# One inverse root moved to GpSimd, a new order of the last part, and first scores ahead of the second head group's projections

## The reference

```
x = x + attn_a(layernorm(x))   # 16 heads of 16; softmax attention for the 307 queries per head
                               # with the largest max(score) - mean(score), zeros for the rest
x = x + ffn(layernorm(x))      # router picks 4 of 16 blocks of 64 hidden channels; relu; biases
x = x + attn_b(layernorm(x))   # rmsnorm, recurrent attention, rmsnorm, gated silu FFN (1024 hidden)
x = x + ffn(layernorm(x))
```

```
S = a_t[..., None] * S + k_t[..., :, None] * v_t[..., None, :]
o_t = einsum('bhk,bhkv->bhv', q_t, S)
mu  = mean(o, -1);  var = mean((o - mu) ** 2, -1)
o   = (o - mu) / sqrt(var + 1e-5)
out = (o * silu(x @ wog.T + bog)) @ wo.T
```

## Time and profile before

| | us |
|---|---|
| median of 3 runs (1687.06 to 1697.72) | 1687.17 |
| the profiled execution, its own time | 1679.56 |
| its span in the trace | 1677.8 |
| PE busy | 1477.8 (88%) |
| DVE busy | 1113.6 (66%) |
| ACT busy | 663.8 (40%) |
| POOL busy | 551.7 (33%) |
| mean granted clock of PE | 0.953 of full |

### The profile page before, as it was taken

The page is one execution under the profiler, slowest core; times in us unless marked ns, Lnnn a source line. Parts: engine busy times, 40 slices in busy tenths (PEclk is TensorE's granted clock), DMA queues, the critical chain, the costliest instruction groups (busy, mean ns, idle before and its releaser), DMA issues.

```text
span 1677.8 us, 25200 instructions
## 1 busy us (share of the span) xinstructions
PE 1477.8 (88%) x8675; PEld 1047.4 (62%) x8724; DVE 1113.6 (66%) x2180; ACT 663.8 (40%) x924; POOL 551.7 (33%) x697
## 2 busy tenths in 40 slices
PE   3688898898898649999988799999999999997898
PEld 2333343343343238888877587878777887876787
DVE  3887778877877775655557667677585857574533
ACT  1275666666675602322232333334333332332111
POOL 5344534544642011422221322332232322331320
PEclk9698999999999959999999999999999999998899
DMA  5222312322222030011010010101010000100000
GB/s 149 51 56 56 69 42 57 66 57 54 58 55 57 2 128 26 26 38 51 26 34 13 13 26 1 38 1 38 0 38 0 25 13 8 29 0 13 13 1 26
DMA packets 56413, 61.03 MB, mean 36 GB/s; under 512 B 15733, under 2 KB 41637, under 8 KB 56349
## 3 DMA queue, kind: packets, MB, share of 16 engines
q1 hardware_dynamic: 42653, 43.89, 10.1%
q0 software_dynamic: 13408, 16.29, 4.6%
q10 hardware_dynamic: 288, 0.00, 0.0%
HBM read 25.51 MB, written 8.90 MB: 21 GB/s over the span
## 4 chain that ended last, share of the span: by engine, by line
PE 50%; issue 23%; DVE 12%; POOL 9%; ACT 4%; DMA 1%; POOLq 0%; DVEq 0%; SPq 0%; another core or an unknown queue 0%; ACTq 0%
PE ps L1790 12%; PE ps L1818 9%; PE ps L810 6%; PE ps L783 4%; PE ps L797 3%; PE ps L744 3%; POOL h L1395 3%; DVE mc L497 3%; PE ps L1801 2%; PE ps L752 2%; POOL kT L1368 2%; PE ps L1776 1%; ACT pT0a L671 1%; PE ps L1830 1%; DVE race L601 1%
## 5 line engine op out<-in xcount | busy, mean ns | idle before, releaser
L497 DVE TENSOR_REDUCE mc<-ps 128x2 f32<-128x1024 f32 x256 | 306.4, 1220 | 45.1 <-PE ps L783 45.1
L1818 PE MATMUL ps<-w_hi,h 128*128 128x256 f32 x1024 | 221.3, 300 | 0.3 <-DVE h L1630 0.3
L250 POOL DMA_DIRECT2D k_st<-k_hi x256 | 123.8, 489 | 266.8 <-PE ps L797 251.4
L1697 ACT ACTIVATE h<-ps 128x512 fp32r<-128x512 f32 x128 | 76.4, 598 | 325.2 <-PE ps L1851 191.9
L1790 PE MATMUL ps<-xT_b,w_hi 128*128 128x512 f32 x512 | 171.1, 415 | 4.3 <-ACT maskT L1691 4.3
L783 PE MATMUL ps<-k_st,q_st 48*128 48x512 f32 x512 | 138.5, 538 | 38.2 <-DVE mc L497 36.5
L1818 PEld LDWEIGHTS ps<-w_hi,h 128*128 128x128 f32 x1024 | 166.6, 190 | 4.9 <-DVE h L1630 3.1
L1630 DVE SCALAR_TENSOR_TENSOR h<-ps,h 128x512 fp32r<-128x512 f32 x128 | 88.3, 691 | 110.8 <-ACT h L1697 109.2
L1395 POOL TENSOR_TENSOR h<-hf,h 128x512 fp32r<-128x512 f32 x56 | 72.5, 1295 | 265.0 <-DVE h L1643 265.0
L783 PEld LDWEIGHTS ps<-k_st,q_st 48*128 48x128 f32 x512 | 52.2, 200 | 170.6 <-issue 86.5
L1818 PE MATMUL ps<-w_lo,h 128*128 128x256 f32 x512 | 143.3, 280 | 0.0
(11 more groups left out here) (266 smaller groups left out, 3388.7 us busy)
## 6 DMA issues: line engine op xcount, KB each, us to landing
q_st<-q_hi SPq DMA_DIRECT2D x256, 32.0 KB, 2.0
k_st<-k_hi POOLq DMA_DIRECT2D x256, 32.0 KB, 2.0
q_st<-q_lo SPq DMA_DIRECT2D x128, 32.0 KB, 2.1
k_st<-k_lo POOLq DMA_DIRECT2D x128, 32.0 KB, 1.9
x<-in_x_dram SPq DMA_DIRECT2D x8, 512.0 KB, 3.9
x_dram<-x SPq DMA_DIRECT2D x8, 512.0 KB, 2.9
yn<-x_dram SPq DMA_DIRECT2D x16, 256.0 KB, 4.5
x<-x_dram SPq DMA_DIRECT2D x16, 256.0 KB, 3.9
```

The lines of the kernel that those rows point to most:

```text
L250: eng.dma_start((q_st, k_st)[which][par][64 * e + DH * r:64 * e + DH * r + DH, j, :].bitcast(F32), src[(2 * j + e) * DH:(2 * j + e + 1) * ...
L497: v.tensor_reduce(mc[par][:, qt, 2 * HU + j:MC:NPAIR], ps[:, at:at + 2, :], AX_X, ALU.max).then_inc(max_done, 1)
L1697: a.activation(h[s][m % 2][0][:, :], ps[:, RING[s] + m % 2, :], ACT.Relu).then_inc(F[s]["relu"], 1)
L1818: last = t_.matmul(ps[:, ACC[s] + t // 2, (t % 2) * D:(t % 2 + 1) * D], h[s][m % 2][a][:, t * P:(t + 1) * P], ws[k][:, m, :], start=m == 0 ...
```

## The change

Three things are changed. First, in the start-up, the scores of the first unit begin right after V of g = 0; Q, K and mean for g = 1 are put behind score tiles 2, 5 and 8 (`EARLY`), on PE and DVE alike; statistics of the second x move on DVE ahead of the low part of K for g = 0, and its normalisation on POOL ahead of the 24 copies into `k_st`. Second, `o.ln`: POOL makes the power -0.5 of all 64 values of a partition in one instruction, with a tile of constants (`mu`, filled once), and the root on ACT and four instructions on DVE go. Third, the list `CLOSE` has a new order; the parts in it are the same.

```diff
+EARLY = [2, 5, 8]
...
     def pool(eng):
...
+        normalise(1, TASKS_FIRST.index("X1"), True)
         eng.wait_ge(dve_init, 2)
         eng.wait_ge(misc_free, 4)
         for j in range(NPAIR):
             stack_one(eng, 1, 0, j, k_in)
-        normalise(1, TASKS_FIRST.index("X1"), True)
...
     def dve(eng):
...
         low(0, 0, 0, 3)
+        for t in range(NT):
+            last = stats(1, t)
+        variance(last)
         low(1, 0, 0, 4)
...
         values(0, TASKS_FIRST.index("V"))
-        low(0, 1, 1, 6)
-        low(1, 1, 1, 7)
-        for t in range(NT):
-            last = stats(1, t)
-        variance(last)
         for n in range(NMS + AHEAD):
             score_max(n, n % 2, n // NMS, n % NMS)
+            if n == EARLY[0]:
+                low(0, 1, 1, 6)
+            if n == EARLY[1]:
+                low(1, 1, 1, 7)
...
     def pe(eng):
...
         v_task(0).then_inc(task_done, 1)
-        eng.wait_ge(misc_free, 5)
-        qk_task(0, 1).then_inc(task_done, 1)
-        eng.wait_ge(misc_free, 6)
-        qk_task(1, 1).then_inc(task_done, 1)
-        eng.wait_ge(misc_free, 7)
-        eng.wait_ge(kmean_ready, 2)
-        mean_task(1).then_inc(task_done, 1)
         for n in range(NMS + AHEAD):
             scores(n, n % 2, n // NMS, 0, n % NMS)
+            if n == EARLY[0]:
+                eng.wait_ge(misc_free, 5)
+                qk_task(0, 1).then_inc(task_done, 1)
+            if n == EARLY[1]:
+                eng.wait_ge(misc_free, 6)
+                qk_task(1, 1).then_inc(task_done, 1)
+            if n == EARLY[2]:
+                eng.wait_ge(misc_free, 7)
+                eng.wait_ge(kmean_ready, 2)
+                mean_task(1).then_inc(task_done, 1)
...
-CLOSE = ["rec7", "o.mean", "o.ln", "o.T", "g.T", "g.m0", "g.u0", "g.m1", "g.u1", "g.d0", "g.m2", "g.u2",
+CLOSE = ["g.T", "rec7", "g.m0", "g.u0", "g.m1", "g.u1", "g.d0", "g.m2", "g.u2", "g.d1", "g.m3", "g.u3",
+        "o.mean", "g.d2", "o.ln", "g.m4", "g.u4", "g.d3", "g.m5", "g.u5", "o.T", "g.d4", "g.m6", "g.u6", "g.d5",
...
     def pool(eng):
...
+        def deviation(i):
+            eng.wait_ge(pads_cleared, 1)
+            power(var[:, :], rs[:, :], mu[:, :], O["var"], O["rs"], i)
...
         def pads(i):
...
+            g.memset(mu[:, :], -0.5)
...
+        parts["o.ln"] = deviation
...
         def o_ln(i):
...
             eng.wait_ge(O["rs"], i + 1)
-            link(v.reciprocal(rs[:, :], rs[:, :]))
-            link(v.scalar_tensor_tensor(mu[:, :], var[:, :], -0.5, rs[:, :], ALU.mult, ALU.mult))
-            link(v.tensor_tensor(mu[:, :], mu[:, :], rs[:, :], ALU.mult))
-            link(v.scalar_tensor_tensor(rs[:, :], mu[:, :], 1.5, rs[:, :], ALU.add, ALU.mult))
             v.tensor_tensor(tokh, tokh, rs[:, :].unsqueeze(2).to_broadcast([P, NT * H, DH]),
...
     def act(eng):
...
-        def deviation(i):
-            eng.wait_ge(O["var"], i + 1)
-            a.activation(rs[:, :], var[:, :], ACT.Sqrt).then_inc(O["rs"], 1)
```

More of the change, by code:

```diff
@@ L52 @@
 DVE_LINKS = 15
-DVE_LINKS_B = 29
+DVE_LINKS_B = 25
 TASKS = [[("V", 0, "E"), ("X0", 0, "L"), ("X1", 1, "E"), ("Q", 2, "E"), ("K", 3, "E"), ("O1", 4, "E"),
@@ L1037 @@
         "f1.end"]
-CLOSE = ["rec7", "o.mean", "o.ln", "o.T", "g.T", "g.m0", "g.u0", "g.m1", "g.u1", "g.d0", "g.m2", "g.u2",
[8 rows of a table removed]
+CLOSE = ["g.T", "rec7", "g.m0", "g.u0", "g.m1", "g.u1", "g.d0", "g.m2", "g.u2", "g.d1", "g.m3", "g.u3",
+        "o.mean", "g.d2", "o.ln", "g.m4", "g.u4", "g.d3", "g.m5", "g.u5", "o.T", "g.d4", "g.m6", "g.u6", "g.d5",
+        "g.m7", "o.x", "z.y", "g.u7", "g.d6", "o.wo", "g.d7", "g.end", "e.rms", "e.x", "f1.ln", "e.gT", "f1.T",
[6 rows of a table added]
 Z_NEXT = Z_START[1:] + steps("z.o", NOUT) + ["og"] + steps("rec", T8)[:CUT]
@@ L1741, in y_squares @@
             last.then_inc(G["ss"], 1)
-        def deviation(i):
-            eng.wait_ge(O["var"], i + 1)
-            a.activation(rs[:, :], var[:, :], ACT.Sqrt).then_inc(O["rs"], 1)
         parts = {"z.ready": lambda i: eng.wait_ge(small_in, 16 * len(small)), "z.y": copied,
-                 "z.T": lambda i: high(z_turn(i, 0), 0, s1), "og": og_silu, "o.mean": o_squares, "o.ln": deviation,
+                 "z.T": lambda i: high(z_turn(i, 0), 0, s1), "og": og_silu, "o.mean": o_squares,
                  "o.wo": y_squares,
```

## The result

| kernel | median us | before in the same comparison | ratio to before [95% interval] |
|---|---|---|---|
| before | 1687.12 | | 1 |
| the changed kernel | 1751.16 | 1687.12 | 1.0369 [1.0314, 1.0424] |

The change makes the kernel slower, by 3.7%, which is 62 us by the ratio. That is outside the range of the prediction (1664 to 1716) and on the side to which it gave 0.21.

A forecast was written before the change was run, and what follows sets the result against it. PE bounds the loop (90.20 of 94.00 us busy), with waits at the start-up and closing part. Terms -3.5 - 3.4 - 9.5 = -16.4 us take the median from 1687.17 to 1670.8; range 1664 to 1716.

The forecast's parts named there:

- Part 2: The root in `o.ln`: with a short power PE's wait of 0.68 us goes in 5 loop passes, -3.4 us.
- I take the lower end: Choice for the power on 64 values: cost above a plain instruction is fixed, so it takes 1.13 us.
- P: Time in us of one POOL power on 128x64, shown by no row; bounds 1.13 and 13.1.
- Rival 1: Power costs by the value, delaying PE beyond P of 2.2; 1717 us at P = 8; chance 0.26 for P above 6.
- the 10 for the clock: Added at P = 13.1: PE falls to its lower level in each pass, some 10 us more.
- once again P - 5: Opening, second `o.ln`: a long power costs PE about P - 5 us, after about P - 3 at the first.
- Part 3: The closing order: PE's waits at the start of the closing part go; -9.5 us, bounds -13 and -6.
- the step back: Closing part, last root mean square: `e.m0` starts later because all of `f1.ln` precedes the split of `e.gT`; +1.9 us.
- the term of -2.1: Start of the closing part: PE's work in the 0.50 stretch runs at the upper clock level instead, -2.1 us.
- the +1.0 for a longer lower level: Closing part, last root mean square: PE stands idle longer, so its lower clock level lasts longer, +1.0 us.
- Part 1: The start-up: DVE's first maximum at about 37.0 instead of 46.71; -3.5 us, bounds -6 and 0.
- so I take the early end: Start-up: both new passes taken at PE's upper clock level, so the 16th maximum ends 4.1 us earlier.

The follow-up runs named there:

- Experiment 6: The kernel before plus, behind the rest, a row of GpSimd powers on 4 to 128 values and one product; one run, 1728.34 us.
- experiment 7: The changed kernel with the power on only 32 of the 64 values, the others staying 1; 1700.68 us, 1.0097 of before.
- experiment 5: The changed kernel with the power on only 4 of the 64 values, the others staying 1; 1660.16 us, 0.9861 of before.
- experiment 4: The changed kernel with the old root on ACT and DVE, so new start-up and closing order only; 1665.28 us, 0.9876 of before.
- experiment 2: The kernel before with only the new order of the list CLOSE; 1667.52 us, 0.9892 of before.
- experiment 8: Experiment 4 with the split of e.gT again ahead of f1.ln and f1.T behind e.m1; 1667.88 us, 0.9894 of before.

## Why the prediction was wrong

**Part 2 failed, at one step: "I take the lower end".** The unknown P was bounded rightly, from 1.13 to 13.1 us, and the true value is 10.56. The step that failed is the reading of one row at one size: 0.8 us of the power on 4 values above a plain instruction can be fixed or belong to the values, and I made them fixed since the row "is flat at 1.019". It is flat only because all its instructions have the same size; a row that never varies says nothing on a slope. Experiment 6 put it the other way: 0.64 of the 1.02 us belong to the 4 values. What kept the result in doubt was known beforehand: beyond P = 2.2 everything goes to PE, so the two ends of the bound lay 100 us apart, and the chance of 0.26 for P above 6, and a range cut at P = 8, were too narrow for a choice with nothing behind it.

**The estimate from the skill's figures fell with it.** By the 12 cycles an element that the Trainium skill, GPSIMD Engine Reference, § 3.1, gives for code that branches on data, P was an estimated 1.6 us. The runs show 0.159 us a value, an estimated 190 cycles at the page's 1.2 GHz. The page's advice, § 4.1, that elementwise work belongs on VectorE, was right for this change. It gives no figure for a power, and the one that I borrowed is too small for it by 16 times.

**Rival 1 was right as a mechanism.** With P = 10.56 its terms give 41.3 for the loop, 7.6 + 5.6 for the opening and 9.0 for the closing part, with -13.0 for the rest +50, 1737 us, and with the 10 for the clock 1747; measured 1751.16. That the last sum comes so near is partly luck: with the -20.9 measured for parts 1 and 3 in place of -13.0 it gives 1740. (Its terms also break even at P = 4.2 and not at 4.4.) By its formula PE's wait in a pass is 0.68 + 10.56 - 2.3 = 8.9; it is 9.10. What was too small is the clock: 17.6 us of busy time up to the seventh scaling alone, not 10 in all. In the opening the waits are 8.09 and 8.02 us, so the second was not the shorter one that "once again P - 5" had made it; in experiment 7 the two are 2.20 and 2.91 us.

**The rest of part 2 was right.** With a short power (experiment 5) the wait goes and a pass is 1.1 us shorter, of which 0.68 were forecast. Against experiment 4, whose pass is as long as that of before, PE's idle time falls from 3.59 to 2.88 us (windows above), and that is the 0.68. The other 0.4 us are busy time of PE in the 4 us around the wait; why they go is open. The window of before shows 3.80 us of idle time, 0.2 more, only because its trace lacks the records of three matmuls a pass (527 instead of 530). One of them stands in what looks like a longer wait, in before and in experiment 4:

```profile
1204.85 0.66 PE L1888 MATMUL ps<-tok,head_sum 128*128 128x128 f32 x4 [0.51 <-ACT maskT L1691]
```

```profile
1201.65 0.39 PE L1857 MATMUL ps<-maskT,expand 128*128 128x512 bf16 x1 [0.28 <-ACT maskT L1697]
1201.88 0.67 PE L1894 MATMUL ps<-tok,head_sum 128*128 128x128 f32 x4
```

**Part 3 was right in kind and too small.** Forecast -9.5, bounds -13 and -6; -13.5 in the trace, -18 in time with an interval from -24 to -12. Waits: -10.3 and +1.9, together -8.4, forecast, -10.8 measured: the three waits of 10.56 went whole, the step back was 1.0 and not 1.9, and the rest are waits of 0.3 us and less. Clock: the term of -2.1 came, but the +1.0 for a longer lower level behind the root mean square didn't: it lasts 13.7 us in before, in two stretches, and 13.7 in experiment 2, in one, and busy time fell by 2.7.

**Part 1 was about right in time and wrong in its steps.** Forecast -3.5; measured -4 with an interval that reaches 0, so the agreement may be luck. The first maximum came at 38.8 and not at 37.0: the copies landed 4.85 us after issue where I had charged 2.0 and 0.6 for the x that travels ahead of them. The waits between maxima came to 8.5 us with the low parts (2.95, 4.4 and 1.1 above a maximum's length), the upper end of my 5.3 to 8.4, because PE was at its lower level from 29.4 to 49.9 us. The step that failed there is "so I take the early end": it read the clock's level at 36.67 from one trace of before, and experiment 2, with the same old start-up, is at 0.50 from 28.9 us on. (By the sum's own numbers the early end was 4.4 us earlier, not 4.1.)

## What to carry to other kernels

A duration at one size is one point, and not a line: when an operation moves to a shape that the trace does not show, either end of the bound may be true, and if the ends lie on both sides of the break-even point, the chances must say so, or a measurement at two sizes comes first. When an in-order engine waits for a long instruction elsewhere, count the wait on the path and then add the clock that PE loses during and behind it, here a quarter of the loss. Before a difference between two traces is explained, compare how many records each has for the same work. Test the parts of a change apart: two of the three together gained 1.2% and were hidden under the third.

## What the runs showed of the hardware

- GpSimd's `pow` on float32 took 0.38 us and 0.159 us a value of a partition, from 4 to 128 values, the same for bases 0.37, 1 and 12345 and exponents -0.5 and 2; the product of 64 values took 0.31 us (experiment 6).
- Stretches of PE at 0.50 differ from one execution of identical code to the next, and even from pass to pass: a loop pass without long waits took 93.85 us or 95.4 us, the latter with a low stretch of some 3.4 us in it (experiment 2), and the old start-up ran at a mean clock of 0.79 or 0.65.
- A wait of 9.1 us in each pass came with 10.2 us at 0.50 at its end and behind it, one of 4.0 us with 3.4 us behind it (the changed kernel and experiment 7).
- A shorter wait is not always a gain: with 1.56 instead of 2.54 us of wait the lower level lasted as long, 13.7 us, but PE worked for 10.5 instead of 8.1 us of it (experiments 8 and 4).
